# More split couples in a three-layer interaction network, and a longer ring for their high parts

## The chip, the cores and the metric

The kernel runs on one core of a Trainium2 chip. The core has a matmul engine (TensorE, PE in the profile; its weight loads are PEld), three engines for elementwise work (VectorE or DVE, ScalarE or ACT, GpSimd or POOL) and a queue that issues DMAs (SyncE or SP). The metric is the time of one execution on the device in microseconds (us); several executions are timed and their median is given.

## What is computed

A compressed interaction network (CIN) over 512 examples with 39 fields of dimension 16 and three layers of 128 maps:

```python
for idx, (W, b) in enumerate(params):
    z = jnp.einsum('bhd,bkd,hks->bsd', x0, xk, W) + b[None, :, None]
    z = jax.nn.relu(z)
    if idx != n_layers - 1:
        half = z.shape[1] // 2
        xk = z[:, :half, :]
        direct.append(z[:, half:, :])
    else:
        direct.append(z)
logit = jnp.sum(jnp.concatenate(direct, axis=1), axis=-1)
```

x0 is always the input. Layer 0 multiplies it with itself, layers 1 and 2 with the 64 maps of the layer before. Everything is float32.

## The kernel before

**Tiles.** The 512 x 16 columns are worked in 16 chunks of 512 columns. For a chunk each layer is a long contraction over products of two fields: VectorE writes products of up to 128 rows by 512 columns (a tile), TensorE multiplies each tile by its 128 x 128 weights and adds to the layer's accumulator z. Two tiles are a couple, and one VectorE instruction makes the products of a couple (line 259). Layer 0 has 7 tiles of 117 rows (the last 78), so 4 couples, the last of one tile; layers 1 and 2 have 20 tiles each, 10 couples.

**Kinds.** A couple is multiplied in one of two ways. An *exact* couple (kind E) goes to TensorE as float32, in two matmul instructions a tile. A *split* couple goes as float32r, a form that keeps fewer bits and is multiplied in one instruction: its products are rounded by ScalarE to a high part (hi, line 478), the rest (products minus hi) is a low part (lo), and three passes a tile are added up: hi by w_hi, hi by w_lo and lo by w_hi. The weights are split likewise, once, at the start. In the last tile of layers 1 and 2 the second pass is left out, since its w_lo shares the rows of w_hi. The low part is made by GpSimd (kind S, products in the ring `raw` in SBUF, line 370) or by VectorE (kind D, products in `d_raw` in PSUM, a single slot, line 272). KINDS (line 28) gives the kind of every couple: before, 9 exact and 15 split couples a chunk, 12 of them S and 3 D.

**Order.** All engines run the same rounds, one a chunk: layer 1 of chunk c, layer 0 of chunk c + 1, layer 2 of chunk c. Layer 0 of chunk 0 goes ahead of the rounds, the last round has no layer 0. The first and last round are written out, the others are a loop of 7 turns with two rounds each. Since the loop unrolls two rounds, every ring's length has to divide twice the number of couples a round that use it (asserted at line 79). `place` (line 82) gives the number of a couple in its ring.

**VectorE** (from line 237) multiplies the couples in order. The low part of a D couple k is made after the product of k + 2 (D_LAG, line 262); it waits for the couple's high part and for a free low slot. The sum of the direct half over the 16 dimensions, `sum_direct`, is put into layer 2 after eight couples (SUM_DIRECT_AT = 8, line 54), `sum_last` of the chunk before into layer 1 after seven. Products of layer 2 wait for the maps of layer 1 (`z1_evacuated`).

**ScalarE** (from line 465) makes the high parts in the order of the split couples. Between them it does the relus: `spread_maps(1)` after layer 0's high parts, `copy_fields` and `finish_last` in layer 1, and in layer 2 the maps of layer 0 that the next round's layer 1 needs:

```python
for m, k in enumerate(split_of(2)):
    if m == MAPS1_AT and more:
        act.wait_ge(lo_used, place("SD", i, d, 2)[0])
        act.wait_ge(direct_summed, c + 1)
        spread_maps(0, maps1, direct[0:HALF, :], z0_evacuated)
    split_hi(2, i, d, [k], more)
```

MAPS1_AT is 6 (line 57), and m counts split couples, not couples. The wait for `direct_summed` is there because `direct` is one buffer, and the relu writes into it what the next sum reads.

**GpSimd** (from line 358) makes the low parts of the S couples in order; each waits for its high part and for a low slot (a ring of three, shared with the D couples, freed by TensorE with `lo_used`).

**TensorE** (from line 388) takes each layer's couples in order, the low part of a couple two couples later (`schedule`, LO_LAG), the last split couple's at the end.

**SyncE** loads the fields and the spread fields of the chunk after next as soon as VectorE has multiplied the couples that read them.

Of the kernel before, what the change touches and what calls it, by code (L numbers as in the profile page):

```python
# [24 lines left out]


E, S, D = "E", "S", "D"
KINDS = ("EDEE", "SESSSESDES", "SESSESSDES")
COUPLES = tuple(len(k) for k in KINDS)
assert KINDS[0][-1] == E and KINDS[1][-1] == S and KINDS[2][-1] == S  # L30


def split_of(layer):

    return [k for k in range(COUPLES[layer]) if KINDS[layer][k] != E]

# [4 lines left out]
D_LAG = 2  # L41
for _kinds in KINDS:
    assert all(D not in _kinds[k + 1:k + 1 + D_LAG] and k + D_LAG < len(_kinds)
# [2 lines left out]

EXACT_RING = 3
RAW_RING = 4
HI_RING = 5
LO_RING = 3  # L50


# [10 lines left out]
def tiles_of(layer, kind):  # L63

    tiles = (TILES0, TILES, TILES)[layer]
    return [t for t in range(tiles) if (KINDS[layer][t // 2] == E) == (kind == E)]

# [4 lines left out]
def count_kind(kinds, kind):  # L72

    return sum(k in kind for k in kinds)


PER_ROUND = {kind: sum(count_kind(kinds, kind) for kinds in KINDS) for kind in (E, S, D, "SD")}
for _ring, _kind in ((EXACT_RING, E), (RAW_RING, S), (HI_RING, "SD"), (LO_RING, "SD")):
    assert 2 * PER_ROUND[_kind] % _ring == 0


def place(kind, i, d, layer, k=0, more=True):

    at = {1: 0, 0: count_kind(KINDS[1], kind), 2: count_kind(KINDS[1], kind) + more * count_kind(KINDS[0], kind)}
    first = count_kind(KINDS[0], kind) + PER_ROUND[kind] * d + at[layer] + count_kind(KINDS[layer][:k], kind)
    if d < 0:
        first = count_kind(KINDS[0][:k], kind)
    return first + 2 * PER_ROUND[kind] * i, first  # L90


def cin_kernel(nc, x_fields, x_spread, w0e, w0s, w1e, w1s, w2e, w2s, b, out):
# [11 lines left out]
    with ctx:  # L105
        def sb(name, shape, dt=fp32):
            return ctx.enter_context(nc.sbuf_tensor(name, shape, dt))
# [17 lines left out]
        raw = sb("raw", [128, RAW_RING, 2, COLS])  # L125
        hi = sb("hi", [128, HI_RING, 2, COLS], fp32r)
        lo = sb("lo", [128, LO_RING, 2, COLS], fp32r)
# [110 lines left out]
        def _(dve):  # L238
# [26 lines left out]
            def split_lo_couple(layer, counts):  # L265
# [4 lines left out]
                if slot >= LO_RING:  # L270
                    dve.wait_ge(lo_used, count - LO_RING + 1)
                nc.vector.tensor_tensor(lo[0:rows, slot % LO_RING, :, :], d_raw[0:rows, :, :],  # L272
                                        hi[0:rows, slot % HI_RING, :, :].bitcast(fp32),
                                        ALU.subtract).then_inc(d_lo_ready, 1)
# [84 lines left out]
        def _(pool):  # L359
            def split_lo(layer, i, d, more=True):  # L360

                rows = ROWS0 if layer == 0 else 128
                for k in range(COUPLES[layer]):
                    if KINDS[layer][k] == S:
# [3 lines left out]
                        if slot >= LO_RING:  # L368
                            pool.wait_ge(lo_used, count - LO_RING + 1)
                        nc.gpsimd.tensor_tensor(lo[0:rows, slot % LO_RING, :, :],  # L370
                                                raw[0:rows, raw_slot % RAW_RING, :, :],
                                                hi[0:rows, slot % HI_RING, :, :].bitcast(fp32),
                                                ALU.subtract).then_inc(s_lo_ready, 1)
# [15 lines left out]
        def _(pe):  # L389
# [12 lines left out]
            def contract(layer, i, d, more=True):  # L402
# [3 lines left out]
                for step, (what, k) in enumerate(order):  # L406
# [11 lines left out]
                    else:  # L418
                        pe.wait_ge(s_lo_ready if kind == S else d_lo_ready, place(kind, i, d, layer, k, more)[0] + 1)
                    e, h, l = (slot % ring for ring in (EXACT_RING, HI_RING, LO_RING))  # L420
                    passes = []
# [44 lines left out]
        def _(act):  # L466
            def split_hi(layer, i, d, couples, more=True):

                rows = ROWS0 if layer == 0 else 128
                for k in couples:  # L470
# [3 lines left out]
                    act.wait_ge(raw_ready if kind == S else d_raw_ready, kind_count + 1)  # L474
                    if slot >= HI_RING:
                        act.wait_ge(lo_used, count - HI_RING + 1)
# [119 lines left out]
```

## Time and profile before

| | us |
|---|---|
| median of 3 runs | 597.0 (594.65 to 597.07) |
| profiled execution | 594.9 |
| its span | 593.1 |

| engine | busy us | share of the span | instructions |
|---|---|---|---|
| PE (matmul) | 569.8 | 96% | 1952 |
| DVE | 509.5 | 86% | 471 |
| ACT | 339.8 | 57% | 372 |
| POOL | 453.4 | 76% | 196 |

The span is what the profiler saw from the first to the last instruction. L259 means line 259 of the kernel. A matmul's duration overlaps the next one's, so the cost of one is read from start to start. The granted clock (PEclk) is a share of TensorE's full 2.4 GHz.

### The profile page before, as it was taken

Reading aid. Unit: us, or ns where it says so; the run is one execution under the profiler, and the core shown is the slowest. Engines: PE = TensorE matmul, PEld = TensorE weight load, DVE = VectorE, ACT = ScalarE, POOL = GpSimd, SP = SyncE. Lnnn points to the kernel's source line nnn. Section 1 sums busy time; section 2 is a strip of 40 time slices with the busy share of each in tenths; the row PEclk is TensorE's granted clock in tenths of the full one; section 3 lists DMA queues with packets and bytes.
Section 4 is the critical chain, followed back from the end, with each engine's and each line's share of the span. In section 5 each row is a group of like instructions: output and inputs, shape, how many; then the busy total and the mean of one; then the engine's idle time right before and its main releaser. Section 6 shows DMA issues by size and latency. Waiting matters only on the chain.

```text
span 593.1 us, 7442 instructions
## 1 busy us (share of the span) xinstructions
PE 569.8 (96%) x1952; PEld 370.0 (62%) x1952; DVE 509.5 (86%) x471; ACT 339.8 (57%) x372; POOL 453.4 (76%) x196
## 2 busy tenths in 40 slices
PE   2699999999999999999999999999999999999977
PEld 0366666666666666666666666766666666666644
DVE  2789999898889989888998989989898998988853
ACT  1556567474755747576474656647465574747542
POOL 0268969698796969969696896969779696987965
PEclk9999999999999999999999999999999999999989
DMA  8939985380926629083571918448092653900000
GB/s 311 421 138 371 421 331 225 143 353 5 369 120 236 259 105 384 6 335 160 204 291 59 385 50 291 204 167 328 22 384 88 253 242 133 362 1 0 1 2 35
DMA packets 17406, 121.55 MB, mean 205 GB/s; under 512 B 2058, under 2 KB 2058, under 8 KB 5108
## 3 DMA queue, kind: packets, MB, share of 16 engines
q1 hardware_dynamic: 16992, 120.59, 52.0%
q10 hardware_dynamic: 404, 0.84, 0.5%
q8 instruction: 4, 0.07, 0.0%
q14 instruction: 6, 0.05, 0.0%
HBM read 120.90 MB, written 0.52 MB: 205 GB/s over the span
## 4 chain that ended last, share of the span: by engine, by line
PE 95%; DMA 2%; ACT 1%; DVE 1%; issue 0%; ACTq 0%
PE z L435 95%; DMA field_spread<-w0s 2%; ACT hi L478 1%; DVE raw L259 0%; ACT maps L493 0%; DVE d_raw L259 0%; DVE sums L305 0%; ACT z L501 0%; ACTq L526 0%; DVE field_spread L341 0%; ACTq L536 0%
## 5 line engine op out<-in xcount | busy, mean ns | idle before, releaser
L370 POOL TENSOR_TENSOR lo<-raw,hi 128x1024 fp32r<-128x1024 f32 x192 | 453.2, 2394 | 134.2 <-ACT hi L478 119.6
L478 ACT ACTIVATE hi<-raw 128x1024 fp32r<-128x1024 f32 x192 | 203.2, 1059 | 123.0 <-DVE raw L259 118.2
L435 PE MATMUL z<-exact,w_exact 128*128 128x512 f32 (+2 forms) x544 | 260.1, 603 | 10.3 <-DVE exact L259 10.3
L259 DVE TENSOR_TENSOR raw<-field_spread,maps 128x1024 f32<-128x1024 f32 x192 | 228.2, 1217 | 27.4 <-ACT maps L493 27.4
L435 PE MATMUL z<-hi,w_hi 128*128 128x512 f32 (+1 forms) x480 | 209.8, 437 | 9.1 <-ACT hi L478 9.1
L435 PE MATMUL z<-hi,w_lo 128*128 128x512 f32 (+1 forms) x448 | 178.0, 397 | 0.0
L435 PE MATMUL z<-lo,w_hi 128*128 128x512 f32 (+1 forms) x480 | 177.6, 462 | 0.0
L435 PEld LDWEIGHTS z<-exact,w_exact 128*128 128x128 f32 (+2 forms) x544 | 104.7, 193 | 93.8 <-issue 71.6
L435 PEld LDWEIGHTS z<-lo,w_hi 128*128 128x128 f32 (+1 forms) x480 | 90.4, 188 | 53.0 <-issue 38.1
L435 PEld LDWEIGHTS z<-hi,w_hi 128*128 128x128 f32 (+1 forms) x480 | 90.6, 189 | 42.5 <-issue 19.6
L259 DVE TENSOR_TENSOR exact<-field_spread,maps 128x1024 f32<-128x1024 f32 x96 | 116.7, 1216 | 0.0
L435 PEld LDWEIGHTS z<-hi,w_lo 128*128 128x128 f32 (+1 forms) x448 | 84.6, 189 | 29.5 <-issue 11.5
L272 DVE TENSOR_TENSOR lo<-d_raw,hi 128x1024 fp32r<-128x1024 f32 (+1 forms) x48 | 58.6, 1221 | 37.2 <-PE z L435 37.2
L478 ACT ACTIVATE hi<-d_raw 128x1024 fp32r<-128x1024 f32 (+1 forms) x48 | 49.3, 1026 | 70.3 <-DVE d_raw L259 69.0
L493 ACT ACTIVATE maps<-z,bias 64x512 f32<-64x512 f32 x64 | 41.6, 650 | 35.5 <-PE z L435 34.3
L259 DVE TENSOR_TENSOR exact<-fields,copies 117x1024 f32<-117x1024 f32 (+1 forms) x48 | 48.3, 1035 | 0.0
L259 DVE TENSOR_TENSOR d_raw<-field_spread,maps 128x1024 f32<-128x1024 f32 x32 | 39.2, 1223 | 0.0
L495 ACT ACTIVATE direct<-z,bias 64x512 f32<-64x512 f32 x32 | 21.9, 684 | 0.8
L259 DVE TENSOR_TENSOR d_raw<-fields,copies 117x1024 f32<-117x1024 f32 x16 | 19.6, 1223 | 0.0
L305 DVE TENSOR_REDUCE sums<-z 128x512 f32 (+1 forms) x16 | 11.0, 687 | 5.7 <-ACT z L501 5.5
L501 ACT ACTIVATE z<-z,bias 128x512 f32<-128x512 f32 x16 | 10.6, 662 | 6.4 <-PE z L435 6.0
L488 ACT ACTIVATE copies<-fields 117x512 f32<-117x512 f32 x16 | 9.6, 602 | 7.1 <-DMA fields<-x_fields 6.7
(11 smaller groups left out, 22.4 us busy)
## 6 DMA issues: line engine op xcount, KB each, us to landing
field_spread<-x_spread SPq DMA_DIRECT2D x80, 1024.0 KB, 7.6
fields<-x_fields SPq DMA_DIRECT2D x16, 1280.0 KB, 7.1
fields<-x_fields SPq DMA_DIRECT2D x16, 768.0 KB, 4.5
field_spread<-w1s SPq DMA_DIRECT2D x1, 896.0 KB, 12.8
field_spread<-w2s SPq DMA_DIRECT2D x1, 896.0 KB, 17.8
field_spread<-w0e ACTq DMA_DIRECT2D x1, 585.0 KB
out<-sums SPq DMA_DIRECT2D x2, 256.0 KB, 2.1
w_exact<-w1e SPq DMA_DIRECT2D x1, 384.0 KB, 13.3
```

The source lines that it names most:

```text
L259: nc.vector.tensor_tensor(ring, spread[0:rows, 2 * k:2 * k + tiles, :], by[0:rows, :].unsqueeze(1).to_broadcast([rows, tiles, COLS]), ALU. ...
L272: nc.vector.tensor_tensor(lo[0:rows, slot % LO_RING, :, :], d_raw[0:rows, :, :], hi[0:rows, slot % HI_RING, :, :].bitcast(fp32), ALU.subtr ...
L305: nc.vector.tensor_reduce(sums[:, 1, bass.ds(c * EXAMPLES, EXAMPLES)], z[2][:, :].rearrange("p (b d) -> p b d", d=DIM), AX.X, ALU.add).the ...
L370: nc.gpsimd.tensor_tensor(lo[0:rows, slot % LO_RING, :, :], raw[0:rows, raw_slot % RAW_RING, :, :], hi[0:rows, slot % HI_RING, :, :].bitca ...
L435: mm = nc.tensor.matmul(z[layer][:, :], w[0:rows, :], part[0:rows, :], start=(step == 0 and p == 0), stop=(step == len(order) - 1 and p == ...
L478: nc.scalar.activation(hi[0:rows, slot % HI_RING, :, :], products, ACT.Copy).then_inc(hi_ready, 1)
L488: nc.scalar.activation(copies[0:ROWS0, :], field_copies[0:ROWS0, :], ACT.Copy).then_inc(copies_ready, 1)
L493: nc.scalar.activation(maps[half * HALF:(half + 1) * HALF, :], z[n][0:HALF, :], ACT.Relu, bias=bias[0:HALF, n:n + 1]).then_inc(evacuated, 1)
L495: nc.scalar.activation(direct_out, z[n][HALF:OUT, :], ACT.Relu, bias=bias[HALF:OUT, n:n + 1]).then_inc(evacuated, 1)
L501: nc.scalar.activation(z[2][:, :], z[2][:, :], ACT.Relu, bias=bias[:, 2:3]).then_inc(z2_evacuated, 1)
```

## The change

KINDS has other letters: layer 0 is SSEE in place of EDEE; layers 1 and 2 are both SSEDSSSDES in place of SESSSESDES and SESSESSDES. There are now 6 exact and 18 split couples a round, 14 S and 4 D. Per layer the split couples are 2, 8 and 8 in place of 1, 7 and 7; layer 0 has two S couples and no D couple, layers 1 and 2 have two D couples each (k = 3 and 7) in place of one. The high ring has six slots in place of five, 4 KB more a partition. The sizes and orders that follow from KINDS follow it by themselves: the split of the weights, the schedule of TensorE, the places in the rings, and the couple at which ScalarE's and VectorE's other work stands in the order. The constants MAPS1_AT, SUM_DIRECT_AT, LO_LAG and D_LAG and the other rings are as before.

```diff
-KINDS = ("EDEE", "SESSSESDES", "SESSESSDES")
+KINDS = ("SSEE", "SSEDSSSDES", "SSEDSSSDES")
 COUPLES = tuple(len(k) for k in KINDS)
 EXACT_RING = 3
 RAW_RING = 4
-HI_RING = 5
+HI_RING = 6
 LO_RING = 3
```

## Rows read from the trace of the kernel before

**Rows 1.** The page, part 1: busy us, share of the span, instructions.

```profile
PE 569.8 (96%) x1952; PEld 370.0 (62%) x1952; DVE 509.5 (86%) x471; ACT 339.8 (57%) x372; POOL 453.4 (76%) x196
```

**Rows 2.** Stretches: two rounds; start:end, length, busy by engine, clock, DMA.

```profile
219.29:254.38 35.09, 35.09 (x124) 22.95 (x122) 31.47 (x30) 20.94 (x24) 28.35 (x12) 1.00 0.54 208
254.38:289.46 35.08, 35.08 (x124) 22.96 (x122) 31.47 (x29) 20.93 (x24) 28.31 (x12) 1.00 0.54 210
```

**Rows 3.** Timeline of TensorE: start, duration, operation, tiles, count; layers 2, 0, 2.

```profile
231.88 0.40 PE L435 MATMUL z<-hi,w_hi 128*128 128x512 f32 x1
...
234.21 1.88 PE L435 MATMUL z<-exact,w_exact 128*128 128x512 f32 x4
...
236.39 0.39 PE L435 MATMUL z<-hi,w_hi 128*128 128x512 f32 x1
...
252.73 1.88 PE L435 MATMUL z<-exact,w_exact 117*128 117x512 f32 x4
...
258.43 0.39 PE L435 MATMUL z<-hi,w_hi 128*128 128x512 f32 x1
```

**Rows 4.** Timeline of VectorE in layers 1 and 2; in brackets the idle time before.

```profile
246.78 1.22 DVE L272 TENSOR_TENSOR lo<-d_raw,hi 128x1024 fp32r<-128x1024 f32 x1 [1.58 <-PE z L435]
...
254.38 1.22 DVE L259 TENSOR_TENSOR raw<-field_spread,maps 128x1024 f32<-128x1024 f32 x1 [1.25 <-ACT maps L493]
...
263.43 0.68 DVE L299 TENSOR_REDUCE sums<-direct 128x512 f32 x1
...
267.17 1.22 DVE L272 TENSOR_TENSOR lo<-d_raw,hi 128x1024 fp32r<-128x1024 f32 x1 [0.80 <-PE z L435]
268.31 1.21 DVE L259 TENSOR_TENSOR raw<-field_spread,maps 128x1024 f32<-128x1024 f32 x1
```

**Rows 5.** Timeline of GpSimd: runs of low parts in the steady loop.

```profile
234.61 16.52 POOL L370 TENSOR_TENSOR lo<-raw,hi 128x1024 fp32r<-128x1024 f32 x7 [0.94 <-PE z L435]
256.93 11.81 POOL L370 TENSOR_TENSOR lo<-raw,hi 128x1024 fp32r<-128x1024 f32 x5 [5.80 <-ACT hi L478]
```

**Rows 6.** Timeline of ScalarE in the second half of layer 2.

```profile
263.64 1.02 ACT L478 ACTIVATE hi<-d_raw 128x1024 fp32r<-128x1024 f32 x1
264.69 1.33 ACT L493 ACTIVATE maps<-z,bias 64x512 f32<-64x512 f32 x2
266.04 0.69 ACT L495 ACTIVATE direct<-z,bias 64x512 f32<-64x512 f32 x1
266.75 1.06 ACT L478 ACTIVATE hi<-raw 128x1024 fp32r<-128x1024 f32 x1
```

**Rows 7.** Timeline of the start: TensorE's first work, two rows of ScalarE.

```profile
10.33 3.78 PE L435 MATMUL z<-exact,w_exact 117*128 117x512 f32 x4 [10.33 <-DVE exact L259]
15.43 0.79 PE L435 MATMUL z<-hi,w_hi 117*128 117x512 f32 x1 [1.32 <-ACT hi L478]
...
16.44 0.63 PE L435 MATMUL z<-hi,w_hi 117*128 117x512 f32 x1
...
17.30 4.03 PE L435 MATMUL z<-exact,w_exact 117*128 117x512 f32 x6
...
20.76 1.03 PE L435 MATMUL z<-lo,w_hi 117*128 117x512 f32 x2
21.90 1.32 ACT L493 ACTIVATE maps<-z,bias 64x512 f32<-64x512 f32 x2 [4.94 <-PE z L435]
...
24.51 1.06 ACT L478 ACTIVATE hi<-raw 128x1024 fp32r<-128x1024 f32 x1 [0.58 <-DVE raw L259]
25.71 0.47 PE L435 MATMUL z<-hi,w_hi 128*128 128x512 f32 x1 [3.92 <-ACT hi L478]
```

**Rows 8.** Last layer 2: timeline rows of TensorE and ScalarE, stretches as in rows 2.

```profile
572.59 0.55 PE L435 MATMUL z<-hi,w_hi 128*128 128x512 f32 x1 [3.85 <-ACT hi L478]
...
589.21 0.66 ACT L501 ACTIVATE z<-z,bias 128x512 f32<-128x512 f32 x1 [5.98 <-PE z L435]
...
573.50:574.50 1.00, 1.00 (x4) 0.81 (x3) 1.00 (x2) 0.85 (x1) 1.00 (x1) 0.50 0.07 16
...
576.50:577.50 1.00, 1.00 (x5) 0.65 (x4) 1.00 (x2) 0.46 (x1) 1.00 (x2) 1.00 0.00 0
```

## The prediction

> **What bounds the kernel now.** I read the busy line of the page first [rows 1]: TensorE is busy 96% of the span, VectorE 86%, GpSimd 76%, ScalarE 57%. The table of stretches says whether that 96% is a real bound: two rounds of the steady loop, cut at VectorE's first product of layer 2, take 35.09 and 35.08 us and TensorE is busy in all of it [rows 2]. The timeline of TensorE then gives the two prices. From 231.88 to 234.21 stand eight hi and two lo passes, so a pass of a split tile costs 2.33/10 = 0.233 us. From 234.21 to 236.39 stand four instructions of an exact couple and two lo passes, so the couple costs 2.18 - 0.47 = 1.71 us and an exact tile 0.857 us [rows 3]. A round has 88 passes (41 in each of layers 1 and 2, 6 in layer 0) and 17 exact tiles (6, 6, 5): 88 x 0.233 + 17 x 0.857 = 20.50 + 14.57 = 35.07 us, the measured round. So TensorE never waits in a steady round, and the others have slack: VectorE waits three times a round, 1.25 us for the maps of layer 2 and 0.80 us for a low slot in layer 2 [rows 4] and 1.58 us for one in layer 1 [rows 4], 3.63 in all.
>
> **What the change gives TensorE.** A split tile costs three passes, 0.699 us, against 0.857 for an exact one: 0.158 us less. Six tiles a round change over: 6 x 0.158 = 0.95 us, and the round's work becomes 106 x 0.233 + 11 x 0.857 = 24.70 + 9.43 = 34.13 us (layers 1 and 2: 47 passes and 4 exact tiles, 14.38 each; layer 0: 12 passes and 3 exact tiles, 5.37). Over 16 chunks that is 15.1 us, if TensorE stays the one that never waits.
>
> **What it costs the others.** VectorE multiplies 24 couples as before and makes one more low part, 1.14 us from one start to the next [rows 4]. It worked 35.09 - 3.63 = 31.46 us a round and would work 32.6 of 34.13. GpSimd makes 14 low parts in place of 12; one takes 2.36 us (11.81/5) [rows 5], so 33.1 of 34.13. ScalarE makes three more high parts of 1.08 us, 20.9 + 3.2 = 24.1 us. Each fits by its total, so totals don't settle it; order does. The ring of six is forced by 36 high parts in two rounds, which five doesn't divide; by my timetable below no high slot is waited for with five or six, so I cost it at nothing. Its cover is the 2 us and more by which each slot comes free.
>
> **The order in layer 2.** I set t = 0 at VectorE's first product of layer 2, and T where TensorE ends layer 1. T is 252.73 and t = 0 is 254.38 [rows 3, 4], so t = 0 is T + 1.65: the two relus of the maps (1.35) and the signals. TensorE does layer 0 in between: before 5.70 us (252.73 to 258.43), after 5.37, so it enters layer 2 at t = 3.72.
> The line MAPS1_AT = 6 stays. It counts split couples, and that is what moves. Before, the seventh split couple of layer 2 is k = 9, so ScalarE makes the high part of k = 7 (263.64), then the maps of layer 1 and the direct half (264.69 and 266.04), then the high part of k = 9 (266.75) [rows 6]. After, split couples are 0, 1, 3, 4, 5, 6, 7, 9: the seventh is k = 7. The maps are now queued on ScalarE *ahead* of the high part of k = 7, and they wait for the sum of the direct half on VectorE, which comes only after the product of k = 7, behind one low part more than before.
> Step by step, from products at 1.13 us (254.38 to 263.43 is eight of them) [rows 4]: eight products and the low part of k = 3 are 9.05 + 1.14, so the sum starts at t = 10.19 and ends at 10.87. ScalarE starts the maps at 10.97; 1.35 + 0.71 later (264.69 to 266.75 in [rows 6]) it starts the high part of k = 7 at 13.03, done 14.05. TensorE takes it 0.14 later, as after 24.51 + 1.06 it started at 25.71 [rows 7]: t = 14.19.
> TensorE wants it earlier. In its order there stand before it: high parts 0, 1, 3, 4, 5, 6 (24 passes), low parts 0, 1, 3, 4 (8 passes) and the exact couple 2: 32 x 0.233 + 1.71 = 9.17, so it is there at 3.72 + 9.17 = 12.89. **It waits 1.30 us in every round**, more than the 0.95 it gained. Before, the same pass had slack: its high part was done at t = 10.28.
> After that: 15 passes and an exact couple to the end of layer 2, 3.50 + 1.71 = 5.21, then layer 1, 14.38: T' = t 33.78. The next t = 0 is 1.65 later, so the round is **35.43 us** in place of 35.09. It repeats itself as long as VectorE is done with layer 0 by then. Its low part of k = 7 also waits for that high part (14.15 in place of 13.05), layer 1 then starts at t = 15.3, and adding ten products, two low parts, a sum of 0.60 and a wait of 0.5 for a low slot, layer 0 starts at 29.9 and ends at 34.0. It has 1.4 us left.
>
> **GpSimd in layer 1.** The one new wait here: low part 4 of layer 1 takes the slot of low part 0, which TensorE frees when it has used it. TensorE is through with that at t = 19.4 + 8 x 0.233 + 1.71 + 0.47 = 23.4. GpSimd starts 0.4 us after such a release (the passes before the exact couple at 234.21 end its wait at 234.61) [rows 3, 5]: 23.8, and four low parts of 2.36 later it ends at 33.3. TensorE wants the last of them at 33.8 - 0.47 = 33.3. So it comes about 0.1 late and the round is some 35.5. Queued behind it are layer 0's two low parts, which end at 38.0, that is t = 2.5 of the next round; TensorE wants the second at 3.3, and GpSimd's first of layer 2 is ready at 2.55 (256.93 - 254.38) [rows 4, 5]. Tight everywhere, with no loss by itself.
>
> **Start and end.** The first couple of the program is now a split one. TensorE started at 10.33 with an exact couple and had its first high part at 15.43 [rows 7]; now nothing runs before the summed and split weights, so it starts at some 15.4 with all of layer 0. The passes there cost (17.30 - 16.44)/2 = 0.43 us each, near twice 0.233; the six exact instructions behind them took 3.46 us (17.30 to 20.76), between 6 x 0.429 = 2.57 at the fast price and twice that, so the clock rose among them, at about 19. If it rises at 19 again, 8.4 of the 12 passes are done by then, and 3.6 x 0.233 + 3 x 0.857 = 3.4 more end layer 0 at 22.4, where it ended at 21.8; with all of it at the slow price it ends at 15.4 + 12 x 0.43 + 3 x 1.71 = 25.7. So it costs 0.6 to 4; I take 0.6, since the work before the clock rose in the old run was no denser. In round 0 VectorE also splits the weights of layer 2 ahead of t = 0, so its first hold-up is about 1.0 longer. The last layer 2, which has no maps behind it, gains 14.70 - 14.38 = 0.3 (47 passes and 4 exact tiles for 41 and 6).
>
> **The sum.** 15 rounds of 35.5 in place of 35.09 are +6.2; start +0.5, round 0 +1.0, end -0.3: +7.4. Made against the profiled execution, whose span is 593.1 and time 594.9, that is a span of 600.5 and 602.3 us. The median of the three runs is 597.0, 2.1 above that execution. I say 603.0, between 602.3 and 604.4.
>
> **The rivals.**
> *TensorE keeps the bound.* For it: every total fits in 34.13 us. It needs the high part of k = 7 by t = 12.9, that is the sum on VectorE 1.3 us earlier than its queue allows. Time: 594.9 - 15.1 + 0.6 = 580.4. Chance 0.08. Half a hold-up (0.6 us a round, if signals or the maps take less than I read) gives 580.4 + 15 x 0.65 = 590, and up to 598 where three quarters or more of it stay: 0.10, half of it under 594.
> *The clock falls in every hold-up.* At the end TensorE waited 3.85 us and then ran at a granted clock of 0.50, the 1.2 GHz level, at 573.5 and again the full one at 576.5 [rows 8]; layer 2 took 16.4 us (572.59 to 0.2 before the relu at 589.21) in place of 41 x 0.233 + 6 x 0.857 = 14.7. The 1.7 us lost, 15 times over, give 603 + 25 = 628. Against it: the wait is 1.3 us in 35, not 3.9, and the rows show no fall after a wait that short. The one wait of 1.32 us, before 15.43, lies where the passes were slow already [rows 7]. [...] Chance 0.08. The Trainium skill speaks for this rival: "TensorE: Matmul & The Clock Gate", section "A second HAM failure mode: psum-queue depth-cycling", tells of short idles between groups of matmuls, frequent enough that the clock goes to and fro. No steady round of this trace has such idles, so no row agrees or disagrees; by that rule the time would be the 628 above.
> *GpSimd becomes the bound.* Its 33.1 us plus the start after a low slot's release. If each low part costs 0.03 more, or TensorE wants the last one 0.3 earlier, the round grows by 0.2 to 0.5: 606 to 611. It decides where four low parts and a release take longer than the 9.9 us that TensorE needs from low part 0 to the last. Chance 0.12.
> The ring of five or six makes no difference in any of them.
>
> **How the numbers follow.** Forecast, 599 to 606: 0.62, of it 0.55 above 600. TensorE bound 0.08, half a hold-up 0.10, GpSimd 0.12, clock 0.08. The range 593 to 611 holds 0.62 + 0.12 + 0.05 = 0.79. A measurement here can tell some 0.5%, 3 us, from no change. Slower by more (over 600): 0.55 + 0.12 + 0.08 = 0.75. Within: 0.07 + 0.05 = 0.12. Faster (under 594): 0.08 + 0.05 = 0.13.
>
> **What would show it.** Right: in the trace of after TensorE waits for a high part on ScalarE once a round, about 1.3 us, at the seventh split couple of layer 2; the maps stand before that high part on ScalarE; rounds are 35.4 to 35.5 us; VectorE's low part of k = 7 waits for ScalarE. TensorE's work without that wait is 34.1. GpSimd is busy over 92% of a round. Wrong: rounds of 34.1 and no such wait (the hold-up is hidden); a granted clock under 1 in steady rounds (the clock); TensorE waiting for GpSimd by over 0.3 us (GpSimd).

## The result and the profile after

The kernel after takes 608.75 us (median of 4, 607.91 to 609.05) against 595.84 for the kernel before on the same chips: 1.022 times as long, interval 1.019 to 1.025. Its profiled execution has a span of 606.1 us, 13.0 above 593.1. The direction is the forecast one and the time lies in the range of 593 to 611. But it lies above 606, where the forecast itself ended, and 5.6 us of the span were not forecast.

The page, part 1 (busy us, share of the span, instructions), to be read against [rows 1]:

```profile
PE 560.9 (93%) x2048; PEld 387.2 (64%) x2048; DVE 533.8 (88%) x487; ACT 386.7 (64%) x420; POOL 532.9 (88%) x228
```

TensorE is busy 8.9 us less, though each of the three others is busy 24 to 80 us more, and the span is longer: TensorE now waits. Two steady rounds, in the columns of [rows 2], cut at TensorE's start after its wait:

```profile
242.39:277.95 35.56, 34.51 (x129) 23.91 (x129) 32.60 (x30) 23.80 (x27) 33.24 (x15) 1.00 0.51 208
277.95:313.44 35.49, 34.52 (x129) 23.92 (x129) 32.59 (x30) 23.80 (x27) 33.12 (x15) 1.00 0.51 206
```

35.56 and 35.49 us, where [rows 2] has 35.09, and one microsecond of each without a matmul in flight. The timelines of VectorE, ScalarE and TensorE around that wait (start, duration, operation, in brackets the idle time before), to be read against [rows 4] and [rows 6]:

```profile
263.85 2.35 DVE L259 TENSOR_TENSOR raw<-field_spread,maps 128x1024 f32<-128x1024 f32 x2 [1.55 <-ACT maps L493]
...
272.90 1.22 DVE L259 TENSOR_TENSOR d_raw<-field_spread,maps 128x1024 f32<-128x1024 f32 x1
274.04 0.68 DVE L299 TENSOR_REDUCE sums<-direct 128x512 f32 x1
...
278.02 1.22 DVE L272 TENSOR_TENSOR lo<-d_raw,hi 128x1024 fp32r<-128x1024 f32 x1 [1.04 <-ACT hi L478]
```

```profile
273.10 1.06 ACT L478 ACTIVATE hi<-raw 128x1024 fp32r<-128x1024 f32 x1 [1.21 <-DVE raw L259]
274.81 1.33 ACT L493 ACTIVATE maps<-z,bias 64x512 f32<-64x512 f32 x2 [0.65 <-DVE sums L299]
276.16 0.69 ACT L495 ACTIVATE direct<-z,bias 64x512 f32<-64x512 f32 x1
276.87 1.02 ACT L478 ACTIVATE hi<-d_raw 128x1024 fp32r<-128x1024 f32 x1
```

```profile
276.27 0.63 PE L435 MATMUL z<-lo,w_hi 128*128 128x512 f32 x2
277.95 0.50 PE L435 MATMUL z<-hi,w_hi 128*128 128x512 f32 x1 [1.05 <-ACT hi L478]
```

With t = 0 at 263.85: the sum at t = 10.19, the maps at 10.96, the high part of k = 7 at 13.02, TensorE at 14.10 (forecast: 10.19, 10.97, 13.03, 14.19). By its price of 0.233 us a pass TensorE was through with the two low passes at 276.74, so it lost 1.21 us. (The bracket gives 1.05, since it counts from the modelled end of the last matmul; the waits in brackets below are all counted so.) ScalarE stands idle 0.65 us with the high part of k = 7 behind it in its queue and its products ready since 274.12.

Where most of the other 5.6 us went is seen in the start. VectorE's split of layer 2's weights, and what follows it, before and after:

```profile
42.56 1.88 DVE L314 TENSOR_TENSOR w_lo<-field_spread,w_hi 128x1664 fp32r<-128x1664 f32 x1
44.47 0.29 DVE L318 TENSOR_TENSOR w_hi<-field_spread,w_hi 64x128 fp32r<-64x128 f32 x1
44.79 1.22 DVE L259 TENSOR_TENSOR raw<-field_spread,maps 128x1024 f32<-128x1024 f32 x1
```

```profile
44.67 3.64 DVE L314 TENSOR_TENSOR w_lo<-field_spread,w_hi 128x1920 fp32r<-128x1920 f32 x1
48.34 2.33 DVE L318 TENSOR_TENSOR w_hi<-field_spread,w_hi 64x128 fp32r<-64x128 f32 x1
50.71 2.35 DVE L259 TENSOR_TENSOR raw<-field_spread,maps 128x1024 f32<-128x1024 f32 x2
```

The second instruction is the same in both, 64 rows by 128 columns, and takes 0.29 us in one and 2.33 in the other. What differs is GpSimd beside it. Before, GpSimd had made its last low part from 37.74 to 40.11 and had none until 47.18. After, it works through, and its own six low parts take 16.08 us and not 6 x 2.36 = 14.2:

```profile
34.45 16.08 POOL L370 TENSOR_TENSOR lo<-raw,hi 128x1024 fp32r<-128x1024 f32 x6 [2.69 <-PE z L435]
```

Layer 1's weights meet the same: their split, from 18.40, takes 4.04 us for 1920 columns beside a GpSimd low part that ends at 20.43, and took 1.88 for 1664 before, when GpSimd had no work yet. That one is hidden, since VectorE then waits 1.89 us for the maps.

TensorE feels the weights of layer 2 twice, at the end of layer 0 and at the start of layer 2, which it starts at 53.16; before, it was at 47.85:

```profile
50.58 0.73 PE L435 MATMUL z<-lo,w_hi 117*128 117x512 f32 x2 [0.93 <-POOL lo L370]
53.16 0.47 PE L435 MATMUL z<-hi,w_hi 128*128 128x512 f32 x1 [1.85 <-ACT hi L478]
```

Behind these two waits the granted clock fell: it was 0.50 from 54 to 57, and full there before. That cost little in this kernel, because TensorE is ahead of the high part of k = 7 all the same and only waits less for it (0.66 us in this round, about 1.0 in the steady ones).

The span's 13.0 us, cut at VectorE's first product of layer 2 in round 0 and in the last round (44.79 and 570.13 before, 50.71 and 583.48 after): +5.92 up to the first, +7.43 between them (15 rounds), -0.35 behind.

### The profile page after: what moved, and what is told of

It reads as the page before. It is cut to its first block, busy times and chain, and to the rows that moved or that the text cites. A ratio compares the mean times of both kernels' runs of the same rounds, so it can differ in the third digit from the quotient of the medians.

```text
span 606.1 us, 7952 instructions
## 1 busy us (share of the span) xinstructions
PE 560.9 (93%) x2048; PEld 387.2 (64%) x2048; DVE 533.8 (88%) x487; ACT 386.7 (64%) x420; POOL 532.9 (88%) x228
## 4 chain that ended last, share of the span: by engine, by line
PE 55%; DVE 20%; issue 12%; ACT 8%; DMA 2%; DVEq 1%; ACTq 0%
PE z L435 55%; DVE raw L259 8%; DVE d_raw L259 6%; ACT maps L493 4%; DVE lo L272 3%; ACT hi L478 3%; DMA field_spread<-w0s 2%; ACT direct L495 2%; DVE sums L299 1%; DVE exact L259 1%; DVE w_lo L314 1%; DVEq L253 0%; DVE w_hi L318 0%; DVEq L249 0%; DVEq L257 0%
## 5 line engine op out<-in xcount | busy, mean ns | idle before, releaser
L370 POOL TENSOR_TENSOR lo<-raw,hi 128x1024 fp32r<-128x1024 f32 (+1 forms) x224 | 532.6, 2411 | 68.3 <-ACT hi L478 40.9
L478 ACT ACTIVATE hi<-raw 128x1024 fp32r<-128x1024 f32 (+1 forms) x224 | 235.5, 1059 | 125.1 <-DVE raw L259 121.3
L435 PE MATMUL z<-hi,w_lo 128*128 128x512 f32 (+1 forms) x544 | 218.6, 402 | 0.0
L435 PE MATMUL z<-lo,w_hi 128*128 128x512 f32 (+1 forms) x576 | 215.4, 464 | 0.9 <-POOL lo L370 0.9
L435 PE MATMUL z<-exact,w_exact 128*128 128x512 f32 (+2 forms) x352 | 168.7, 598 | 0.0
L272 DVE TENSOR_TENSOR lo<-d_raw,hi 128x1024 fp32r<-128x1024 f32 x64 | 78.2, 1222 | 23.6 <-ACT hi L478 15.2
L478 ACT ACTIVATE hi<-d_raw 128x1024 fp32r<-128x1024 f32 x64 | 65.8, 1027 | 43.6 <-DVE d_raw L259 43.1
L259 DVE TENSOR_TENSOR d_raw<-field_spread,maps 128x1024 f32<-128x1024 f32 x64 | 78.2, 1222 | 0.0
L259 DVE TENSOR_TENSOR exact<-field_spread,maps 128x1024 f32<-128x1024 f32 x64 | 77.7, 1213 | 0.0
L259 DVE TENSOR_TENSOR raw<-fields,copies 117x1024 f32<-117x1024 f32 x32 | 37.6, 1213 | 0.0
```

The lines of the kernel that those rows point to most:

```text
L259: nc.vector.tensor_tensor(ring, spread[0:rows, 2 * k:2 * k + tiles, :], by[0:rows, :].unsqueeze(1).to_broadcast([rows, tiles, COLS]), ALU. ...
L370: nc.gpsimd.tensor_tensor(lo[0:rows, slot % LO_RING, :, :], raw[0:rows, raw_slot % RAW_RING, :, :], hi[0:rows, slot % HI_RING, :, :].bitca ...
L435: mm = nc.tensor.matmul(z[layer][:, :], w[0:rows, :], part[0:rows, :], start=(step == 0 and p == 0), stop=(step == len(order) - 1 and p == ...
L478: nc.scalar.activation(hi[0:rows, slot % HI_RING, :, :], products, ACT.Copy).then_inc(hi_ready, 1)
```

## The experiments

**The maps one split couple later.** If the hold-up is the whole loss of a round, moving the maps behind the high part of k = 7 gives it back.

```diff
-MAPS1_AT = 6
+MAPS1_AT = 7
```

> The kernel after with MAPS1_AT = 7: the maps of layer 0 stand on ScalarE behind the high part of k = 7 again and ahead of that of k = 9, as in the kernel before. Queue theory (the 1.2 us hold-up of TensorE at the high part of k = 7 is the whole loss of a steady round): no wait of TensorE on ScalarE in a steady round, rounds of 34.15 to 34.4 us in place of 35.52, span 606.1 - 15 x 1.2 = 588, time near 590, below both kernels. GpSimd theory (its 14 low parts are the real bound, and would take over): rounds of 34.8 or more, span 596 or more, TensorE waiting on GpSimd.

Measured: 592.25 us, 0.9975 of the kernel before (0.9956 to 0.9993); measured once more, 592.02, 0.9954 (0.9936 to 0.9971). Span 589.8. A steady round by TensorE's end of layer 1, and ScalarE in it:

```profile
290.93:325.25 34.32, 34.32 (x129) 23.92 (x128) 32.57 (x30) 23.81 (x27) 33.15 (x15) 1.00 0.52 214
```

```profile
302.77 1.03 ACT L478 ACTIVATE hi<-d_raw 128x1024 fp32r<-128x1024 f32 x1
303.82 1.32 ACT L493 ACTIVATE maps<-z,bias 64x512 f32<-64x512 f32 x2
305.17 0.69 ACT L495 ACTIVATE direct<-z,bias 64x512 f32<-64x512 f32 x1
305.88 1.06 ACT L478 ACTIVATE hi<-raw 128x1024 fp32r<-128x1024 f32 x1
```

TensorE has no wait in a steady round. Rounds take 34.3 and 34.4 us in turn, 34.38 on average, and nearly all of the 1.2 us a round is back. So the hold-up was the loss of a steady round, and this version is slightly faster than the kernel before. The span is 589.8 and not the 588 forecast. The round is 0.2 above the 34.13 of TensorE's passes, and that is still GpSimd: the four last low passes of layer 1 and of layer 2 take 1.01 us each time (from 289.72 and from 309.55) and not 4 x 0.233 = 0.93. At 33.15 busy us of 34.32 it did not take over, but it is close.

**The sum one couple earlier.** This moves the release of the maps and not their place.

```diff
-SUM_DIRECT_AT = 8
+SUM_DIRECT_AT = 7
```

> The kernel after with SUM_DIRECT_AT = 7: VectorE makes the sum of the direct half before the product of k = 7, not behind it, so 1.13 us earlier; the maps keep their place on ScalarE. Queue theory: the maps can start only when ScalarE is through with the high part of k = 6 (about t = 10.3), so they start 0.65 us earlier and not 1.13; TensorE's hold-up at k = 7 falls from 1.2 to about 0.6, rounds of 34.85 to 34.95 us, span near 597. If the maps' place on ScalarE had nothing to do with it, the rounds stay at 35.52.

Measured: 600.44 us in one run, span 598.6, and the round:

```profile
293.98:328.91 34.93, 34.52 (x129) 23.91 (x128) 32.59 (x30) 23.80 (x26) 33.22 (x15) 1.00 0.54 210
```

The round is 34.93 us, as forecast. The maps then follow the high part of k = 6 with no gap (304.68, then 305.76). So ScalarE's queue sets them and no longer the sum, and 0.59 of the 1.13 us arrive.

**The maps one split couple earlier still.** This is more of the same cause, to size it and to see whether the clock answers to longer waits.

```diff
-MAPS1_AT = 6
+MAPS1_AT = 5
```

> The kernel after with MAPS1_AT = 5: the maps stand ahead of the high part of k = 6 too. Queue theory: that high part is ready at t = 14.05 and TensorE wants it at about 11.5, so the hold-up is 2.7 us in place of 1.3, rounds of 36.9 us, span near 627. Clock theory (longer idle stretches make the granted clock fall): rounds of 38 or more, a granted clock under 1.00 in steady rounds. If the loss were elsewhere: rounds as before, 35.5.

Measured: 638.47 us in one run, span 636.7, and both theories hold at once. From one end of layer 1 to the next, over the 14 rounds behind round 0, eight rounds take 36.9 to 37.0 us, the forecast of the queue alone, and six take 38.3 to 38.5. One of each kind, and inside the second the stretches around its wait:

```profile
162.00:199.00 37.00, 34.61 (x130) 23.95 (x129) 32.60 (x30) 23.75 (x27) 33.28 (x15) 1.00 0.49 198
199.00:237.50 38.50, 36.05 (x130) 25.07 (x129) 32.60 (x30) 23.66 (x27) 33.15 (x15) 0.96 0.47 191
...
213.00:215.00 2.00, 0.50 (x1) 0.47 (x2) 0.50 (x1) 1.95 (x3) 0.60 (x2) 0.89 0.98 401
215.00:217.00 2.00, 2.00 (x6) 1.55 (x5) 0.00 (x0) 1.44 (x2) 1.98 (x1) 0.50 1.04 434
217.00:219.00 2.00, 2.00 (x8) 1.55 (x8) 1.56 (x2) 0.00 (x0) 0.00 (x0) 0.76 0.50 209
219.00:221.00 2.00, 2.00 (x7) 0.99 (x6) 2.00 (x3) 1.07 (x2) 1.73 (x1) 1.00 0.00 0
```

```profile
177.51 0.50 PE L435 MATMUL z<-hi,w_hi 128*128 128x512 f32 x1 [2.39 <-ACT hi L478]
...
214.50 0.76 PE L435 MATMUL z<-hi,w_hi 128*128 128x512 f32 x1 [2.45 <-ACT hi L478]
```

Waits of 2.39 and 2.45 us, nearly the same: behind the first the clock stayed at the full level, behind the second it fell to 0.50, the 1.2 GHz level, for about 3 us, which costs 1.4 to 1.5 us. Six times this is 9 us, nearly all of the difference between 627 and 636.7. So the clock rival of the prediction is a real mechanism. The steady waits of the kernel after (0.97 to 1.05 in brackets) set it off in none of 14 rounds, those of 2.4 us in six of 14. Length alone doesn't decide: in round 0 of this same run a wait of 2.07 us, at 65.28, had no fall behind it. Which waits do isn't explained here.

**The same order in the old kinds.** If putting the maps ahead costs as such, it costs there too.

```diff
 KINDS = ("EDEE", "SESSSESDES", "SESSESSDES")
-MAPS1_AT = 6
+MAPS1_AT = 5
```

> The kernel before with MAPS1_AT = 5, which puts the maps of layer 0 ahead of the high part of k = 7 in the old kinds too. Queue theory: the order alone costs nothing while TensorE comes late enough; in the old kinds the sum ends at t = 9.73, the high part of k = 7 is ready near 13.0 and TensorE wants it at 13.5, so rounds stay 35.09 us and the span 593. If putting the maps ahead of it costs as such, rounds grow by about 1 us and the span to 608.

Measured: 597.45 us in one run, span 595.6, and the round is still the old one:

```profile
289.24:324.33 35.09, 35.09 (x123) 22.96 (x122) 31.46 (x30) 20.84 (x23) 28.36 (x12) 1.00 0.54 209
```

ScalarE waits for the sum there too (0.59 us a round), but TensorE has no wait: the high part of k = 7 is done at 303.54, and TensorE comes for it at 304.21, 0.67 us later. The order costs nothing until the new kinds bring TensorE to k = 7 sooner and the sum later. The 2.5 us of span lie outside the steady rounds. The granted clock was low for longer there, 0.57 from 23 to 31 us (0.79 before) and 0.51 from 573 to 580 (0.77 before), and how long it is low differs between executions of one kernel, as the two of MAPS1_AT = 7 show below.

**The low part of the weights without the second SBUF operand.** For layer 2's weights both instructions read their second operand from PSUM, at the same sizes. This kernel leaves out the low parts of those weights: it subtracts whatever stands in `d_raw`, so its logits are not the network's, and it serves for timing alone.

```diff
+if n == 2:
+    other = d_raw[:, 0, 0:OUT].unsqueeze(1).to_broadcast([128, tiles, OUT])
+    tail = d_raw[HALF:128, 0, 0:OUT]
...
 nc.vector.tensor_tensor(w_lo[n][0:rows, 0:tiles, :], w_staged[n][0:rows, 0:tiles, :],
-                        w_hi[n][0:rows, 0:tiles, :].bitcast(fp32),
-                        ALU.subtract).then_inc(weights_lo, 1)
+                        other, ALU.subtract).then_inc(weights_lo, 1)
...
     nc.vector.tensor_tensor(w_hi[n][HALF:128, tiles, :], w_staged[n][HALF:128, tiles, :],
-                            w_hi[n][HALF:128, tiles, :].bitcast(fp32),
-                            ALU.subtract).then_inc(weights_lo, 1)
+                            tail, ALU.subtract).then_inc(weights_lo, 1)
+if n == 2:
+    dve.wait_ge(weights_lo, WEIGHTS_LO[2])
```

> The kernel after, with the low part of layer 2's weights made from d_raw in PSUM in place of w_hi in SBUF, same sizes (those weights' low parts are wrong; nothing else is left out). Port theory (a VectorE instruction with two SBUF operands waits for GpSimd's running one, and GpSimd for it): the two instructions take about 2.15 and 0.3 us in place of 3.64 and 2.33 while GpSimd works, layer 2's first product starts about 47.2 in place of 50.7, and the span falls by 3 to 3.6 us to about 603. Size theory (1920 columns simply take longer than 1664): they keep 3.6 and 2.3 us and the span stays at 606.

Measured: 605.32 us in one run. VectorE, and GpSimd beside it:

```profile
43.96 2.14 DVE L320 TENSOR_TENSOR w_lo<-field_spread,d_raw 128x1920 fp32r<-128x1920 f32 x1
46.13 0.29 DVE L323 TENSOR_TENSOR w_hi<-field_spread,d_raw 64x128 fp32r<-64x128 f32 x1
...
33.74 14.20 POOL L376 TENSOR_TENSOR lo<-raw,hi 128x1024 fp32r<-128x1024 f32 x6 [1.12 <-PE z L441]
```

The two instructions take 2.14 and 0.29 us with GpSimd at work beside them, and GpSimd's six low parts are back at 14.20. Size is not the cause; the second SBUF operand is. The Trainium skill has the rule ("SBUF — State Buffer", section "Who interferes with whom"): a VectorE instruction with two SBUF inputs and a GpSimd instruction that reads SBUF use one pair of ports, and whoever comes second waits until the other has finished. By this rule the trace agrees: 2.33 us are 2.04 of waiting and 0.29 of work, less than one low part of 2.36, and GpSimd's run is 1.9 us longer, near the 2.14 of the weights' instruction.

The span fell by 2.6 us to 603.5, where 3 to 3.6 was expected, though TensorE started layer 2 of round 0 at 49.24 in place of 53.16 and the high part of k = 7 of that round at 60.56 in place of 64.81, 4.25 us sooner. One round on it was 2.60 sooner (97.70 for 100.30). In between the clock took back what is missing. TensorE had waited 1.98 us for that high part (0.66 in the kernel after), and behind it the granted clock was 0.50 from 62 to 64:

```profile
60.56 0.50 PE L441 MATMUL z<-hi,w_hi 128*128 128x512 f32 x1 [1.98 <-ACT hi L484]
```

```profile
62.00:64.00 2.00, 2.00 (x4) 0.94 (x3) 2.00 (x3) 0.99 (x1) 1.28 (x1) 0.50 1.06 436
```

**A shorter ring.** This asks whether the sixth high slot is worth anything.

```diff
-HI_RING = 6
+HI_RING = 4
```

> The kernel after with a high ring of four slots in place of six. Theory: no high slot is waited for, six is there only because five does not divide 36; with four the latest waits on a slot end within 0.1 us of need, so rounds of 35.5 to 35.6 us, span 606 to 608. Rival: the sixth slot gives back something, then rounds of 36 or more with four.

Measured: 609.29 us in one run, span 607.5, a steady round of 35.48 (35.56 and 35.49 with six). With four ScalarE does wait for a high slot, 99 times and 76 us in all, where with six it never does. So "no high slot is waited for" is false for four slots, and what the theory said of the time holds: none of that waiting reaches TensorE.

**An exact couple first.** On top of MAPS1_AT = 7, to size the start.

```diff
-KINDS = ("SSEE", "SSEDSSSDES", "SSEDSSSDES")
+KINDS = ("ESSE", "SSEDSSSDES", "SSEDSSSDES")
```

> The kernel after with MAPS1_AT = 7 and layer 0 as ESSE in place of SSEE, so that the program's first couple is an exact one again and TensorE starts at about 10.3 us. Theory of the start: layer 0 of chunk 0 ends 1 to 1.5 us earlier than with SSEE, and the time is 1 to 2 us below that of the run with MAPS1_AT = 7 alone; steady rounds the same within 0.05 us. Rival: the start is bounded by the weights' loads and their split, then no difference.

Measured: 588.65 us, 0.9896 of the kernel before (0.9866 to 0.9925). Measured once more, with the kernel of MAPS1_AT = 7 on the same chip:

> The kernel with ESSE and MAPS1_AT = 7 once more, beside the other two of this call: about 588.5 us, steady rounds 34.33.

> The kernel after with MAPS1_AT = 7 once more, on the same chip as the other two: about 591.5 us, 2 to 3.5 us above ESSE, from the start and round 0 alone, since steady rounds are 34.32 in both.

Measured there: 589.0 (0.9884, 0.9843 to 0.9925) against 592.02. Steady rounds are 34.4 in both, so the 3 us come from the start and round 0. But they don't come from where I said. TensorE does start at 9.75 in the first of the two, yet it then waits 3.48 us for the first high part, since the weights for it land when they did. Layer 0 ends half a microsecond earlier and not 1 to 1.5. More is gained from the weights of layer 2 on. In the later ESSE run:

```profile
44.16 2.15 DVE L314 TENSOR_TENSOR w_lo<-field_spread,w_hi 128x1920 fp32r<-128x1920 f32 x1
46.34 2.36 DVE L318 TENSOR_TENSOR w_hi<-field_spread,w_hi 64x128 fp32r<-64x128 f32 x1
48.73 2.35 DVE L259 TENSOR_TENSOR raw<-field_spread,maps 128x1024 f32<-128x1024 f32 x2
```

```profile
43.69 7.25 POOL L370 TENSOR_TENSOR lo<-raw,hi 117x1024 fp32r<-117x1024 f32 x2 [0.23 <-PE z L435]
```

The first of VectorE's two instructions doesn't wait now: it takes 2.15 us and not 3.7, and the two together 4.57 and not 6.08 (43.66 to 49.74 in the MAPS1_AT = 7 run beside it). Here it is GpSimd that waits, whose two low parts take 7.25 us and not 4.7. The second still waits for a low part. The records don't show at what moment the order is settled. Here GpSimd's begins 0.47 us before VectorE's and GpSimd waits, while at layer 1's weights in the kernel after GpSimd's begins 0.37 before (18.03 and 18.40) and VectorE waits.

The granted clock differs as well. With MAPS1_AT = 7 alone TensorE waits twice at the collision, and the clock is 0.51 from 51 to 57:

```profile
49.61 0.73 PE L435 MATMUL z<-lo,w_hi 117*128 117x512 f32 x2 [0.94 <-POOL lo L370]
52.19 0.77 PE L435 MATMUL z<-hi,w_hi 128*128 128x512 f32 x1 [1.85 <-ACT hi L478]
```

With ESSE it waits once, 1.65 us, starts layer 2 at 51.55, and the clock stays full. Of the 1.9 us between these two executions (spans 589.4 and 587.5), TensorE has 0.64 when it starts layer 2, and the other 1.27 when it is through with the next layer 1 (31.74 us later with MAPS1_AT = 7, 30.47 with ESSE). On that stretch the first has no wait and the second one of 0.96 us, for a high part, at 68.38. So the larger part of the gain in these two executions is a fall of the clock that doesn't happen.

**One instruction in place of two.** On top of ESSE and MAPS1_AT = 7, the low part of the last tile is made with the others, and ScalarE copies it into place.

```diff
-rows, tiles = (ROWS0, SPLIT_TILES[0]) if n == 0 else (128, SPLIT_TILES[n] - 1)
+rows, tiles = (ROWS0, SPLIT_TILES[0]) if n == 0 else (128, SPLIT_TILES[n])
...
-if n > 0:
-    nc.vector.tensor_tensor(w_hi[n][HALF:128, tiles, :], w_staged[n][HALF:128, tiles, :],
-                            w_hi[n][HALF:128, tiles, :].bitcast(fp32),
-                            ALU.subtract).then_inc(weights_lo, 1)
...
+nc.scalar.activation(w_hi[n][HALF:128, last, :], w_lo[n][HALF:128, last, :].bitcast(fp32),
+                     ACT.Copy).then_inc(weights_lo, 1)
```

> As the run with ESSE and MAPS1_AT = 7, with the low part of the last weight tile made within the one VectorE instruction that makes the others, and copied into place by ScalarE; so VectorE issues one instruction with two SBUF operands for layer 2's weights and not two. Port theory: the second instruction, 0.29 us of work, took 2.36 because GpSimd had taken its turn in between; that turn falls away, layer 2 starts 1.5 to 2.3 us earlier, span 585.5 to 586.5. Rival: the first instruction then waits for GpSimd instead, or TensorE is late anyway, and the span stays at 587 to 588. Steady rounds 34.3 us either way.

Measured: 589.7 us (0.9901, 0.9862 to 0.9939), span 588.0; no better than the 589.0 beside it. VectorE did gain its 2 us, and TensorE did not:

```profile
44.55 2.28 DVE L314 TENSOR_TENSOR w_lo<-field_spread,w_hi 128x2048 fp32r<-128x2048 f32 x1
46.76 2.34 DVE L259 TENSOR_TENSOR raw<-field_spread,maps 128x1024 f32<-128x1024 f32 x2
...
51.47 0.72 PE L431 MATMUL z<-lo,w_hi 117*128 117x512 f32 x2 [1.59 <-POOL lo L366]
```

TensorE waits 1.59 us for layer 0's last low part of GpSimd (1.65 without this edit), so the products of layer 2, 2 us earlier, are not yet wanted. Later they are of use: the wait of 0.96 us at 68.38 is gone here. But behind the 1.59 us the granted clock was 0.58 from 52 to 55, where it is full with ESSE, and from the start of layer 2 to the end of the next layer 1 TensorE takes 30.53 us (30.47 with ESSE). So the rival was right on the span and on TensorE being late, and left out the clock.

## Why the prediction was right, and where its sum fell short

- *TensorE's price* was right. 34.13 us of work a round were forecast; with the hold-up gone the round is 34.38, of which some 0.2 is GpSimd's.
- *The hold-up* was right in place, mechanism and size: 1.21 us for 1.30, every step of the timetable within 0.1 us. The round is 35.52 on average (64.81 to 562.15 for 14 of them), and 35.5 was forecast.
- *GpSimd's 0.1 us* showed: the four last low passes of layer 1 take from 261.17 to 262.20, 1.03 us in place of 4 x 0.233 = 0.93. Little more came of it: in layer 2 of the next round they take 0.94.
- *Round 0 and the end* were right. From the first product of layer 2 in round 0 to that in round 1 it takes 35.55 us in place of 34.12, +1.43, for which the sum had 0.4 + 1.0; the end gave -0.35 for -0.3. The fall of the clock in round 0 was not foreseen, and it was luck that TensorE was not yet wanted there.
- *The start* is the term that failed: +5.92 us for the +0.5 of the sum (the text above it takes 0.6). VectorE comes to layer 2's weights 2.11 us later (44.67 for 42.56). 1.4 of it is layer 0, whose maps come at 23.29 and not 21.90 [rows 7], where 0.6 was forecast: the sum of its weights started 0.57 later, at 13.32, so TensorE began at 15.89 and not at 15.4, and a pass still cost 0.43 us up to 19.45. (The profile gives the granted clock as 1.00 from 14 to 20 us in both kernels, where a pass cost 0.43. That the clock rose at about 19 is inferred from the prices.) The other 0.7 is layer 1 of round 0 at a granted clock that stayed low longer (0.84 on average from 27 to 46 us; before, 0.91 from 26 to 44). That part may be chance: in two executions of the kernel with MAPS1_AT = 7 the clock was low into the microsecond from 33 in one and from 30 in the other. Then the weights take 6.04 us (44.67 to 50.71) and not 2.23, another 3.81. The prediction names their split only as work ahead of t = 0, without asking what GpSimd does meanwhile. It said of the steady round that GpSimd has two more low parts behind layer 1's, and did not carry that to round 0, where it mattered.
- *The rivals.* "TensorE keeps the bound" is false for this kernel and true for the one with MAPS1_AT = 7. The clock did not fall in a steady round of the kernel after; it did in round 0, and in six rounds with waits of 2.4 us. GpSimd never became the bound. Yet 608.75 us lies in the band of 606 to 611 that the prediction gave to GpSimd, and above the 599 to 606 of its own forecast: the range held because it was wide enough for a rival that did not come true. Had the start been sized right, the sum would have been 12.8 and not 7.4, against 13.0 in the span.

The change bought 0.95 us of TensorE's time a round, which is there to be had. It paid 1.21 a round for a constant that counts split couples and was left at 6, and 5.9 us once at the start, some of it perhaps the clock's chance.

## What to carry to other kernels

- A constant that places one engine's work by a count of something changes its meaning when that count changes. After such an edit, read each engine's queue anew, and for every wait in it ask what stands behind it and who wants that.
- Totals that fit (33 of 34 us on three engines) say that a round is possible, not that it happens; a timetable of one round, from one product to the next, found the hold-up within 0.1 us.
- Work done once at the start is costed with its neighbours too: an instruction can take eight times as long when another engine is no longer idle beside it.

## What the runs showed of the hardware

A VectorE instruction with both operands in SBUF waits for GpSimd's running one: 0.29 us of work took 2.33, and 2.14 took 3.64. It goes the other way too: GpSimd's two low parts took 7.25 us and not 4.7 in the ESSE run. With one operand in PSUM the same VectorE instructions took 0.29 and 2.14 beside a working GpSimd. The prediction did not have this. The steady loop hides it, since every VectorE instruction with two operands has one of them in PSUM there.

TensorE's clock can fall after idle stretches shorter than the 3.85 us of [rows 8]. It did so after 1.98 us once; after 2.4 us in six rounds of fourteen with the same work around it; after 1.59 us once, in the run with one instruction in place of two; and in round 0 of the kernel after, behind waits of 0.93 and 1.85 close together. It stayed full after 1.65 us in the ESSE run and behind the 0.97 to 1.05 us of every steady round of the kernel after. So the length of one wait doesn't tell. A fall in a steady round cost 1.4 to 1.5 us.
